# Attention in a fused block chain: the two mean squares of a batch as pairs of fp32r products of a split vector, in place of one fp32 product each

## What is computed

```python
def _rmsnorm(x):
    return x * jax.lax.rsqrt(jnp.mean(x * x, axis=-1, keepdims=True) + EPS)

def _ada_rmsnorm(x, t, gamma_w, beta_w):
    return gamma * _rmsnorm(x) + beta

x = x + a_alpha * _attention(_ada_rmsnorm(x, t, attn_gamma_w, attn_beta_w), W_q, W_k, W_v, W_o)
return x + f_alpha * _swiglu(_ada_rmsnorm(x, t, ffn_gamma_w, ffn_beta_w), gate_w, hidden_w, out_w, out_b)
```

## Time and profile before

| | before |
|---|---|
| median of 3 runs | 1163.73 us (1163.27 to 1164.36) |
| profiled execution, its time | 1164.16 us |
| its span, first to last instruction | 1162.3 us |
| TensorE busy | 1063.4 us, 91% |
| VectorE busy | 738.1 us, 64% |
| ScalarE busy | 666.8 us, 57% |
| GpSimd busy | 173.2 us, 15% |
| mean granted TensorE clock | 0.951 of full |

### The profile page before, as it was taken

How to read it: one execution, slowest core, us unless ns; L and a number is a source line. 1 busy time by engine, 2 the same in 40 slices (tenths; PEclk the granted TensorE clock), 3 DMA queues, 4 the chain that set the end, 5 groups by cost and what they waited for, 6 DMA issues and landing times.

```text
span 1162.3 us, 16250 instructions
## 1 busy us (share of the span) xinstructions
PE 1063.4 (91%) x5282; PEld 641.8 (55%) x5282; DVE 738.1 (64%) x1196; ACT 666.8 (57%) x891; POOL 173.2 (15%) x204
## 2 busy tenths in 40 slices
PE   4879999999789899999999999996999999999994
PEld 3657677777444343434444343432377778777772
DVE  3746666787567767777777777776445455555543
ACT  4463334463247777777787877665543645455444
POOL 0000001120131223233333332111101000000000
PEclk9789999999959899999999999998599999999997
DMA  9624522002414363544545354534010000000000
GB/s 312 266 86 159 199 87 87 1 1 82 111 47 150 72 175 74 160 89 151 111 122 137 96 138 100 160 73 137 10 30 1 19 1 19 18 18 18 1 19 36
DMA packets 63304, 103.85 MB, mean 89 GB/s; under 512 B 18704, under 2 KB 28432, under 8 KB 62224
## 3 DMA queue, kind: packets, MB, share of 16 engines
q1 hardware_dynamic: 60352, 100.49, 29.4%
q10 hardware_dynamic: 2896, 2.64, 0.9%
HBM read 65.81 MB, written 33.03 MB: 85 GB/s over the span
## 4 chain that ended last, share of the span: by engine, by line
PE 66%; DVE 12%; issue 8%; ACT 5%; POOL 2%; DMA 1%; SPq 1%; DVEq 0%; POOLq 0%; ACTq 0%
PE st_ps L1533 12%; PE st_ps L1420 7%; PE val_ps L1297 7%; PE gate_ps L1297 7%; PE mx_ps L1533 7%; DVE mx L1083 6%; PE av_ps L1410 6%; PE misc_ps L1352 4%; PE misc_ps L1450 3%; PE mx_ps L1365 3%; PE misc_ps L1437 3%; PE y_ps L1307 2%; DVE stage L1093 1%; PE misc_ps L1441 1%; PE gen_ps L1335 1%
## 5 line engine op out<-in xcount | busy, mean ns | idle before, releaser
L1083 DVE TENSOR_REDUCE mx<-mx_ps 128x1 f32<-128x512 f32 x512 | 330.2, 685 | 137.1 <-PE mx_ps L1365 136.9
L1365 PE MATMUL mx_ps<-kring,qring 48*128 48x512 f32 x512 | 211.8, 480 | 13.8 <-DVE mx L1083 10.2
L1420 PE MATMUL st_ps<-qring,kring 50*128 50x512 f32 x512 | 195.4, 464 | 17.1 <-ACT shared L842 7.1
L1420 PEld LDWEIGHTS st_ps<-qring,kring 50*128 50x128 f32 x512 | 81.0, 193 | 175.0 <-issue 114.9
L842 ACT ACTIVATE pbuf<-st_ps 128x1024 f32<-128x1024 f32 x128 | 129.6, 1023 | 53.9 <-PE st_ps L1420 51.6
L842 ACT ACTIVATE shared<-st_ps 128x1024 f32<-128x1024 f32 x128 | 129.1, 1024 | 46.9 <-PE st_ps L1420 45.3
L1365 PEld LDWEIGHTS mx_ps<-kring,qring 48*128 48x128 f32 x512 | 89.3, 192 | 54.0 <-DVE mx L1083 50.3
L1233 DVE TENSOR_TENSOR shared<-st_ps,shared 128x512 f32<-128x512 f32 x64 | 44.2, 690 | 96.9 <-PE st_ps L1533 62.3
L946 ACT ACTIVATE p_hi<-shared 128x512 fp32r<-128x512 f32 x64 | 40.5, 632 | 99.1 <-DVE shared L1233 99.1
L1132 DVE SCALAR_TENSOR_TENSOR h<-val_ps,r,gelu 128x1024 f32<-128x1024 f32 x32 | 41.1, 1284 | 61.0 <-PE val_ps L1297 61.0
L1237 DVE TENSOR_TENSOR p_lo<-shared,p_hi 128x512 fp32r<-128x512 f32 x64 | 47.3, 739 | 48.5 <-ACT p_hi L946 48.5
(11 more groups left out here) (202 smaller groups left out, 2086.2 us busy)
## 6 DMA issues: line engine op xcount, KB each, us to landing
chunk<-in_gen_w SPq DMA_DIRECT2D x8, 2048.0 KB, 8.8
qring<-q_parts SPq DMA_DIRECT2D x64, 192.0 KB, 3.5
kring<-k_parts SPq DMA_DIRECT2D x64, 192.0 KB, 4.6
q_parts<-stage SPq DMA_DIRECT2D x16, 512.0 KB, 2.8
k_parts<-stage SPq DMA_DIRECT2D x16, 512.0 KB, 2.8
xres<-in_xT SPq DMA_DIRECT2D x8, 512.0 KB, 10.5
shared<-in_x SPq DMA_DIRECT2D x8, 512.0 KB, 9.9
q_parts<-stage SPq DMA_DIRECT2D x16, 256.0 KB, 3.0
```

The lines of the kernel that those rows point to most:

```text
L1083: nc.vector.tensor_reduce(mx[h // GH % 2][:, col:col + 1], mx_ps[qt % 2][:], AX, ALU.max).then_inc(S["mx_free"], 1)
L1365: nc.tensor.matmul(mx_ps[qt % 2][:], qring[r:r + QROWS, h // GH, h % GH // 2, qt * P:(qt + 1) * P], kring[r:r + QROWS, h // GH, h % GH // ...
L1420: ins = nc.tensor.matmul(st_ps[half][:, kt % 2], kring[r:r + SROWS, g, i % GH // 2, kt * P:(kt + 1) * P], qring[r:r + SROWS, g, i % GH // ...
```

## The change

Both means are now made from a split of `tmp`. ScalarE copies `tmp` to fp32r (`sum_hi`), VectorE subtracts (`sum_lo`), and TensorE multiplies a constant fp32r copy of the matrix, `mean_r`, first with `sum_lo` and then with `sum_hi`, into the same `misc`. The two parts lie in `stage[0]`, which is free in these steps.

It applies to the mean of `a` in turns 0 to 6 (`has_a and has_p`, 7 times) and to that of `f` in turns 2 to 6 (`has_f and has_a`, 5 times). In the other turns the fp32 product stays. The mean of `a` stays in step 13; both new instructions stand at the head of that step. The mean of `f` moves on TensorE from step 14 to the end of step 15; its new copy and subtraction stand at the head of step 15, and ScalarE's Ln and Exp of it move from the head of step 15 to its end, behind both Exp of the step and the copy of the heads. GpSimd's addition for `f` waits for `suma_lo` where it waited for `suma_ps`. The other edits merge semaphores (`ident` into `consts`, pairs of the layer norm into `added` and `stat`); no instruction changes its place by them.

```diff
+        sum_hi, sum_lo = stage[0][:, 0], stage[0][:, 1]
...
                 if i == 14 and has_f:
                     wait(pool, "sqf", f + 1)
                     if has_a:
-                        wait(pool, "suma_ps", a + 1)
+                        wait(pool, "suma_lo", a)
...
+            act.wait_ge(A["consts"], 2)
+            nc.scalar.activation(mean_r[:], mean_w[:], ACT.Copy)
             act.wait_ge(A["cond_ps"], 1)
...
+                if i == 13 and has_a and has_p:
+                    wait(act, "addA", a + 1)
+                    copy(sum_hi, tmp[:]).then_inc(S["suma_hi"], 1)
+                if i == 15 and has_f and has_a:
+                    wait(act, "addF", f + 1)
+                    copy(sum_hi, tmp[:]).then_inc(S["sumf_hi"], 1)
...
-                if i == 15 and has_f:
+                if i == 15 and has_f and not has_a:
                     log_mean(one(gen, f).rearrange("p a n -> p (a n)"), misc[:], "sumf_ps", f + 1, "lnf")
                     root(one(gen, f).rearrange("p a n -> p (a n)"), f + 1, "lnf", "rf")
...
                 if i in (7, 11, 15) and has_b:
                     evac_heads(b, i // 4 - 1)
+                if i == 15 and has_f and has_a:
+                    log_mean(one(gen, f).rearrange("p a n -> p (a n)"), misc[:], "sumf_ps", f + 1, "lnf")
+                    root(one(gen, f).rearrange("p a n -> p (a n)"), f + 1, "lnf", "rf")
...
+                if i == 13 and has_a and has_p:
+                    wait(dve, "suma_hi", a)
+                    nc.vector.tensor_tensor(sum_lo, tmp[:], sum_hi.bitcast(F32), ALU.subtract) \
+                        .then_inc(S["suma_lo"], 1)
+                if i == 15 and has_f and has_a:
+                    wait(dve, "sumf_hi", f + 1)
+                    nc.vector.tensor_tensor(sum_lo, tmp[:], sum_hi.bitcast(F32), ALU.subtract) \
+                        .then_inc(S["sumf_lo"], 1)
 
                 early = 1 if i in (1, 2, 10) else 2
                 take_maxima(range(early))
...
+                def mean_of_parts(ready, count, name):
+
+                    wait(pe, ready, count)
+                    nc.tensor.matmul(misc[:], mean_r[:], sum_lo, start=True, stop=False)
+                    nc.tensor.matmul(misc[:], mean_r[:], sum_hi, start=False, stop=True).then_inc(S[name], 1)
+
                 if i == 13 and has_a:
                     take_misc("lna", a + 1)
-                    wait(pe, "addA", a + 1)
-                    nc.tensor.matmul(misc[:], mean_w[:], tmp[:], start=True, stop=True).then_inc(S["suma_ps"], 1)
-                if i == 14 and has_f:
+                    if has_p:
+                        mean_of_parts("suma_lo", a, "suma_ps")
+                    else:
+                        wait(pe, "addA", a + 1)
+                        nc.tensor.matmul(misc[:], mean_w[:], tmp[:], start=True, stop=True).then_inc(S["suma_ps"], 1)
+                if i == 14 and has_f and not has_a:
                     take_misc("lnf", f + 1)
                     wait(pe, "addF", f + 1)
                     nc.tensor.matmul(misc[:], mean_w[:], tmp[:], start=True, stop=True).then_inc(S["sumf_ps"], 1)
+                if i == 15 and has_f and has_a:
+                    take_misc("lnf", f + 1)
+                    mean_of_parts("sumf_lo", f + 1, "sumf_ps")
```

More of the change, by code:

```diff
@@ L131, in all_stages @@
         cond_diag = sb(ctx, "cond_diag", [P, 2, NB])
+        mean_r = sb(ctx, "mean_r", [P, P], F32R)
         ident = sb(ctx, "ident", [P, P])
@@ L289, in all_stages @@
             "w_hi w_lo t h gate_done silu hid_done pf p_hi p_lo out_step "
-            "y x4 xsum mean d sq sqsum var ln rstd e fin stored").split()}
+            "y x4 added stat d sq ln rstd e fin stored").split()}
         block = ctx.enter_context(nc.Block())
@@ L957, in _ @@
                     if f == 5 and ends:
-                        wait_ffn(act, "var", b)
+                        wait_ffn(act, "stat", 2 * b)
                         nc.scalar.activation(rstd[:], av_ps[:], ACT.Ln, bias=eps5[:]).then_inc(F["ln"], 1)
@@ L1244, in _ @@
                         nc.vector.tensor_tensor(xsum[:], x_of(b - 1, 0), x_of(b - 1, 1), ALU.add) \
-                            .then_inc(F["xsum"], 1)
+                            .then_inc(F["added"], 1)
                     if f == 3 and ends:
-                        wait_ffn(dve, "mean", b)
+                        wait_ffn(dve, "stat", 2 * b - 1)
                         for k in range(KD):
@@ L1252, in _ @@
                         wait_ffn(dve, "sq", b)
-                        nc.vector.tensor_tensor(xsum[:], fsq[:, 0], fsq[:, 1], ALU.add).then_inc(F["sqsum"], 1)
+                        nc.vector.tensor_tensor(xsum[:], fsq[:, 0], fsq[:, 1], ALU.add).then_inc(F["added"], 1)
                     if f == 6 and ends:
@@ L1496, in _ @@
                         if first and u == 0:
-                            pe.wait_ge(A["ident"], 4)
+                            pe.wait_ge(A["consts"], 8)
                         if first and u == 1:
@@ L1571, in _ @@
                             wait(pe, "oaug", NG * NB)
-                        wait_ffn(pe, "xsum", b)
-                        nc.tensor.matmul(av_ps[:], mean_w[:], xsum[:], start=True, stop=True).then_inc(F["mean"], 1)
+                        wait_ffn(pe, "added", 2 * b - 1)
+                        nc.tensor.matmul(av_ps[:], mean_w[:], xsum[:], start=True, stop=True).then_inc(F["stat"], 1)
                     if f == 5 and ends:
-                        wait_ffn(pe, "sqsum", b)
-                        nc.tensor.matmul(av_ps[:], mean_w[:], xsum[:], start=True, stop=True).then_inc(F["var"], 1)
+                        wait_ffn(pe, "added", 2 * b)
+                        nc.tensor.matmul(av_ps[:], mean_w[:], xsum[:], start=True, stop=True).then_inc(F["stat"], 1)
                     if makes and f or ends and not f:
```

12 lines of the change are left out of this document (6 added, 6 removed).

## The result

The changed kernel takes 1182.05 us (median of 4 runs, 1181.85 to 1185.46) against 1163.9 us of the kernel before, its profiled execution counted in: a ratio of 1.0163 with a 95% interval of 1.0144 to 1.0182, so slower by 1.4 to 1.8%. The forecast was 1174, with 1169 to 1182 as its whole range. The profiled execution took 1181.85 us with a span of 1179.8, 17.5 us more than the span before.

A forecast was written before the change was run, and what follows sets the result against it. TensorE sets the pace, but ScalarE bounds from the middle of step 14 to step 1 of the next turn. 5 x 2.16 = 10.8 us less 0.65 gives +10.1 on 1163.73, so 1174, range 1169 to 1182.

The forecast's parts named there:

- The sign: Whole kernel: slower by over 0.2%, with a chance of 0.92.
- Step 13: Mean of `a`: the pair saves 0.39 us of TensorE, the subtraction delays it 0.3, leaving 0.1 us a turn.
- Step 14: TensorE loses its 1.05 us product for `f`; no gain counted, as ScalarE has no idle time to give.
- Step 15, steps 1 to 5: Copy and locked subtraction delay maxima, second Exp and `h`; TensorE cannot make it up: 2.16 us in each of five turns.
- 2.16: Microseconds more for ScalarE in each turn with both `f` and `a`: 0.52 its new copy, the rest new idle time.
- Rival B: Step 15: GpSimd does not hold VectorE's subtraction up, 0.6 us less a turn, +7.1, so 1171; chance 0.13.
- C: Step 15: GpSimd keeps its port for both `t` products, 1.26 us more a turn, +16.4, so 1180; chance 0.10.
- likeliest case: The main forecast of 1174, own range 1171 to 1177, with the granted clock at 1.00 in turns 2 to 6; chance 0.52.
- rival D: TensorE's waits in steps 15 and 0 also lower the clock, at most 3.5 us a fall: 1177 to 1184; chance 0.17.
- Turn 1: Only the mean of `a`, at half clock: the saving scales to 0.65 us.
- turn 0: Maxima and TensorE feed each other and the subtraction takes 0.6 us of the saving back: nothing gained.
- Rows 11: Profile rows of turn 1 before: 3 us with TensorE busy for 1.85 at full clock, the next stretch at 0.74.

The follow-up runs named there:

- e1: The change with only the mean of `a` split, that of `f` left an fp32 product in step 14: 1164.03 us against 1163.9 before.
- e5: The change plus unread TensorE products, six in the wait of step 15 and five at the end of step 0 of the next turn: 1177.52 us.
- e4: The change with VectorE's subtraction for `f` behind the first two maxima of step 15 instead of ahead of them: 1170.78 us.
- e3: The kernel before, nothing split, with the fp32 product of `f` at the end of step 15 and its Ln and Exp behind the heads' copy: 1169.49 us.
- e8: As e4, with ScalarE's Ln and Exp for the mean of `f` moved to the end of step 0 of the next turn: 1161.2 us.
- e12: As e11, with four unread TensorE products filling the wait of step 15: 1170.57 us.
- e6: The change with GpSimd's two `t` products of step 15 held back until VectorE's subtraction for `f` is done: 1178.18 us.
- e11: The change with only ScalarE's Ln and Exp for `f` moved to the end of step 0 of the next turn: 1184.6 us.
- e2: The change with only the mean of `f` split and moved to step 15, that of `a` left an fp32 product: 1189.59 us.
- e10: The kernel before with Ln and Exp for `f` at the end of step 0 of the next turn and the mean of `a` split: 1161.97 us.

## Why the prediction was wrong, and where it was right

The sign and the chain of waits were right, the clock and with it the size were not: +10.1 us forecast, +17.5 in the span.

*Step 13: size slightly off.* The pair was 0.66 us, as said. The 0.1 us a turn that was to be left of it is nothing (e1), since VectorE's maxima have no idle time left behind its subtraction. Step 14 was right, no gain.

*Step 15, steps 1 to 5: right, and 0.3 us a turn short.* Copy, locked subtraction, maxima, score, second Exp, heads, Ln, Exp, `h` came in the forecast order. `h` starts 11.14 us behind the last Exp of step 13 (582.42 to 593.56); forecast were 10.79 and before 8.57 to 8.64. So 2.5 us a turn against 2.16, over five turns 1.7 us more: the second Exp starts 0.56 us behind the score instead of 0.43, Ln and Exp together take 0.12 more, and the 0.1 of step 13 was not there to take off. e5 shows the 2.5 by itself. Rival B fell (1.41 us, not 0.7), C as well (it would have been 2.5).

*What the 2.16 were made of was half right.* The prediction put them down as 0.52 for ScalarE's copy and 1.6 for idle time. By the experiments the copy is free, since it lies in that idle time (e4 beside e3). The two parts are the order of ScalarE, Ln and Exp behind the wait instead of ahead of it, 1.1 us (e4 to e8, 63.10 to 61.97; e3 alone shows 1.0 to 1.1 too), and the subtraction ahead of the maxima, 1.35 us (e8 to e12, 62.0 to 63.37), half of it GpSimd's hold on the port (0.7, e6). 1.1 and 1.35 are the 2.5 within 0.05.

*The step that failed is the assumption of the likeliest case that the clock stays at 1.00, and with it rival D's size.* D came true, and its 1177 to 1184 hold the time; it had 0.17, with one to three falls of at most 3.5 us each. The bound on the cost of one held, 3.5 us for the longest, though that one lasted 13.6 us and not the 7 that the bound was worked out from; and all five turns fell. From the turn of 64.5 us that the waits alone give, the falls cost 1.0, 0.9, 0, 2.3 and 3.5 us, 7.7 together. A fall of 3.4 us costs 1.35 us where TensorE sets the pace (e11 to e12; also from turn to turn in e2, 65.48, 66.84, 68.16), 0.5 to 0.8 in e3 and e4, and nothing in turn 4 of the change, where it lies beside ScalarE's own chain. The prediction looked at one wait of some 1.3 us, had the row of turn 1 that falls behind such a stretch, and gave the fall 0.17 in spite of it. The wait of step 15 is not only in front of these falls, it brings them about: with that wait filled by products that nobody reads, none of the five turns falls there (e12 beside e11; e5 fills the wait of step 0 too). The Trainium skill tells of a related case (TensorE: Matmul & The Clock Gate, "A second HAM failure mode: psum-queue depth-cycling"): a TensorE that goes through its PSUM tiles with short idle times between its groups of products, often enough, swings between half and full clock. The trace agrees that short waits bring falls; but here it is one wait of 1.14 us for a maxima tile in a turn of 65 us. D had also named the wait of step 0, and rightly: it alone, at 1.6 to 1.9 us, is followed by falls in three of five turns of e3 and of e4.

*The rest.* Turn 1 gave 0.4 instead of 0.65 us, turn 0 gave 0.2, and 2.0 us before them are of the spread between executions. Sum: 12.5 + 7.7 - 0.6 - 2.0 = 17.6, measured 17.5.

Not settled: what decides whether a wait is followed by a fall (turn 3 of e3 has a wait of 1.93 us and none, turn 3 of e6 one of 0.41 us and a fall of 13.7), and why a fall lasts 3.4 us in one turn and 13.6 in another of the same kernel. Rows 11 were ground for a higher chance of a fall, but no row of the kernel before shows how many there would be, or how long. And no version here is shown to beat the kernel before. e8 and e10 have the lowest medians, but their intervals reach to no change, and their turns of 62.0 against 62.05 are worth 0.3 us in all.

## What to carry to other kernels

When an engine waits at one place in every turn, the instructions that stand ahead of that wait cost little and those behind it nearly all of their time (1.24 us of Ln and Exp: 0.26 ahead, 1.0 to 1.1 behind), so before moving a small operation ask which side of the wait it lands on, above all on an engine that shows no idle time only because something fills it. Put an operation that waits on another engine behind the work that others wait for (here the maxima), not ahead of it. And price a new wait of TensorE of a microsecond that comes every turn with a fall of the clock behind it, which here cost between nothing and 3.5 us a turn beside the 2.5 of the waits, and check the granted clock turn by turn before anything else.
